# Loading the first attention head's rows in chunks 13 and 14 of the preparation, its values copied on chip

## What is computed

```python
xn = _layernorm(x)
# attention
q = _rope(split(xn @ Wq + bq)); k = _rope(split(xn @ Wk + bk)); v = split(xn @ Wv + bv)
scores = einsum('bhnd,bhmd->bhnm', q, k) / sqrt(d)
inter = einsum('bhnm,bhmd->bhnd', softmax(scores), v)
attn = inter.transpose(0, 2, 1, 3).reshape(b, n, d) @ Wo + bo
# feed-forward with weights of +1 and -1
h = s0 * (concat([xn, -xn]) @ pm(k0)); h = 2 * relu(h)
h = s1 * (h @ pm(k1)); h = 2 * relu(h)
ffn = s2 * (h @ pm(k2))
return x + attn + ffn
```

## Time and profile before

| | us |
|---|---|
| median of 3 runs | 2652.44 (2651.83 to 2652.5) |
| the profiled execution | 2653.31 |
| its span | 2651.5 |
| the preparation, to the first scores of attention | 0 to 235.6 |
| TensorE busy in the span | 2574.1 (97%) |
| ScalarE busy | 2099.2 (79%) |
| VectorE busy | 977.0 (37%) |
| GpSimd busy | 299.5 (11%) |
| DMA, first tenth of the span | 0.8 to 0.9 busy, 280 to 301 GB/s in the first three slices |
| DMA, later | 0.1 to 0.2 busy |

### The profile page before, as it was taken

How to read it: one execution, slowest core, us unless ns; L and a number is a source line. 1 busy time by engine, 2 the same in 40 slices (tenths; PEclk the granted TensorE clock), 3 DMA queues, 4 the chain that set the end, 5 groups by cost and what they waited for, 6 DMA issues and landing times.

```text
span 2651.5 us, 49117 instructions
## 1 busy us (share of the span) xinstructions
PE 2574.1 (97%) x20679; PEld 1337.6 (50%) x20679; DVE 977.0 (37%) x1669; ACT 2099.2 (79%) x2341; POOL 299.5 (11%) x268
## 2 busy tenths in 40 slices
PE   7887999999999999999999999999999999999997
PEld 5664454544445454545445454545445454545444
DVE  7774233243423332233423332233423332233422
ACT  6885888888888878787887878787887878787883
POOL 6774000000000000000000000000000000000000
PEclk9998999999999999999999999999999999999998
DMA  8995111121212122122212122122212112122203
GB/s 280 301 295 164 41 48 55 45 60 53 58 46 72 46 61 65 52 68 60 77 46 76 47 60 65 52 69 61 77 46 74 49 54 71 51 70 61 77 26 115
DMA packets 235414, 211.83 MB, mean 80 GB/s; under 512 B 146860, under 2 KB 191676, under 8 KB 228792
## 3 DMA queue, kind: packets, MB, share of 16 engines
q1 hardware_dynamic: 226744, 200.29, 25.5%
q10 hardware_dynamic: 8448, 8.39, 1.0%
HBM read 132.06 MB, written 76.55 MB: 79 GB/s over the span
## 4 chain that ended last, share of the span: by engine, by line
PE 89%; issue 1%; DMA 0%; DVE 0%; ACT 0%; SPq 0%; POOLq 0%; POOL 0%; PEldq 0%; ACTq 0%
PE ps_o L1012 36%; PE ps_f L1045 27%; PE ps_s L999 24%; PE ps_y L1058 2%; PE ps_f L1095 0%; DMA probs<-rest_sum_d 0%; PE ps_y L1095 0%; PE ps_o L1095 0%; ACT probs L979 0%; DVE sums L1133 0%; DMA heads_t<-heads 0%; DVE h_lo L1168 0%; POOLq L821 0%; DVE raw L1157 0%; ACT L979 0%
## 5 line engine op out<-in xcount | busy, mean ns | idle before, releaser
L979 ACT ACTIVATE probs<-ps_s 128x1024 f32<-128x1024 f32 x2048 | 1929.8, 1033 | 445.6 <-PE ps_s L999 443.5
L1012 PE MATMUL ps_o<-probs,v_ones 128*32 128x512 f32 x8192 | 1011.4, 600 | 0.0
L999 PE MATMUL ps_s<-q_rows,k_rows 50*128 50x512 f32 x4096 | 868.7, 439 | 6.7 <-SPq L948 5.4
L999 PEld LDWEIGHTS ps_s<-q_rows,k_rows 50*128 50x128 f32 x4096 | 365.9, 184 | 675.6 <-ACT probs L979 601.5
L1012 PEld LDWEIGHTS ps_o<-probs,v_ones 128*32 128x32 f32 x8192 | 201.2, 109 | 417.3 <-issue 294.7
L1045 PE MATMUL ps_f<-h_hi,ffn_w 64*128 64x512 f32 x2048 | 409.2, 393 | 0.0
L1045 PE MATMUL ps_f<-h_lo,ffn_w 64*128 64x512 f32 x2048 | 408.2, 391 | 0.0
L1157 DVE COPY raw<-ps_f 128x512 f32<-128x512 f32 x256 | 164.8, 686 | 560.6 <-PE ps_f L1045 560.6
L1112 POOL TENSOR_TENSOR heads<-heads,sums 128x512 f32<-128x512 f32 x64 | 82.2, 1284 | 2141.0 <-DVE sums L1133 2141.0
L1133 DVE RECIPROCAL sums<-sums 128x128 f32<-128x128 f32 x256 | 226.6, 923 | 1.7
L1045 PEld LDWEIGHTS ps_f<-h_lo,ffn_w 64*128 64x128 f32 x2048 | 198.0, 187 | 34.7
(11 more groups left out here) (105 smaller groups left out, 1376.2 us busy)
## 6 DMA issues: line engine op xcount, KB each, us to landing
k_rows<-k_parts SPq DMA_DIRECT2D x128, 256.0 KB
q_rows<-q_parts SPq DMA_DIRECT2D x384, 64.0 KB
q_parts<-parts SPq DMA_DIRECT2D x32, 512.0 KB, 8.5
k_parts<-parts SPq DMA_DIRECT2D x32, 512.0 KB, 8.5
k_rows<-k_parts SPq DMA_DIRECT2D x128, 128.0 KB
x_chunk<-in_x ACTq DMA_DIRECT2D x16, 512.0 KB, 9.5
xn_d<-xn_t SPq DMA_DIRECT2D x16, 512.0 KB, 9.1
v_heads<-v_sb SPq DMA_DIRECT2D x16, 512.0 KB, 8.1
```

The source lines that it names most:

```text
L979: nc.scalar.activation(probs[:, s % PBUF, half * 2 * C:(half + 1) * 2 * C], ps_s[:, half].rearrange("p c n -> p (c n)"), ACT.Exp, scale=SC ...
L999: last = nc.tensor.matmul(ps_s[:, half, w], k_rows[rows, u, t * P:(t + 1) * P], q_rows[rows, u, half], start=True, stop=True)
L1012: last = nc.tensor.matmul(ps_o[32 * c:32 * c + 2 * DH], v_ones[:, u, t], probs[:, s % PBUF, c * C:(c + 1) * C], start=(t == 0), stop=(t == ...
```

## The change

`FIRST_HEAD_AT` goes from 6 to 13. In chunk 13 SP issues the two zero rows and then all five loads of half 0; in chunk 14 the five loads of half 1 and the load of `xT_lo`. The biases are loaded in chunk 5. The four value loads are gone: at the end of chunks 1 to 4 VectorE copies head 0's values out of `v_sb` into `v_ones`, and ScalarE waits for that copy (`v_kept`) before it writes the `v_sb` buffer again. The memset of ones beside them moves on GpSimd from chunk 6 to chunk 4. The bound is written into another buffer, the second half of `q_rows`, and its four stores are counted on a semaphore of the whole program; the preparation no longer waits for them, attention's SP does, ahead of head 1's loads. ScalarE ends the preparation with an exponential of one column.

```diff
-FIRST_HEAD_AT = 6
+FIRST_HEAD_AT = 13
+        bound_fill = w["q_rows"][:, 1, 0, 0:FILL]
@@ prepare, SP
             def load_first(c):
                 if c == FIRST_HEAD_AT:
                     sp.wait_ge(k_rows_set, 1)
-                at = c - FIRST_HEAD_AT
-                if 0 <= at < LOADS - 2:
-                    load_rows(sp, scratch, 0, w["q_rows"][:, 0], w["k_rows"][:, 0], first_loaded, only=at)
-                if at == 1:
                     for w_half in range(2):
-                        row_of_bound(1, w_half, zero_row)
-                if at == 2:
-                    sp.wait_ge(ones_set, 1)
-                if at % 2 == 0 and 2 <= at < 2 + 2 * CB:
-                    r = at // 2 - 1
-                    v_src = scratch["v"].rearrange("c p (h t d) -> c p h t d", h=H, t=TT)
-                    sp.dma_start(w["v_ones"][:, 0, r * TT:(r + 1) * TT, 0:DH], v_src[r, :, 0]).then_inc(first_loaded, 16)
-                if at == 3:
+                        row_of_bound(1, fill[:], w_half, zero_row)
+                if FIRST_HEAD_AT <= c < FIRST_HEAD_AT + 2:
+                    load_rows(sp, scratch, 0, w["q_rows"][:, 0], w["k_rows"][:, 0], first_loaded, only=c - FIRST_HEAD_AT)
+                if c == FIRST_HEAD_AT + 1:
+                    sp.dma_start(w["xT_lo"][:].bitcast(F32).rearrange("p k n -> p (k n)"), scratch["xn"][0]).then_inc(first_x_loaded, 16)
+                if c == FFN_WEIGHTS_AT + 1:
                     sp.dma_start(bv[:], a["bv"].rearrange("(k p) -> p k", p=P), allow_slow_non_contiguous=True).then_inc(bias_loaded, 16)
                     sp.dma_start(bo[:], a["bo"].rearrange("(o n) -> o n", o=1).broadcast_to([P, D])).then_inc(bias_loaded, 16)
-                if at == 5:
-                    sp.dma_start(w["xT_lo"][:].bitcast(F32).rearrange("p k n -> p (k n)"), scratch["xn"][0]).then_inc(first_x_loaded, 16)
...
-                row_of_bound(0, w_half, bound_row)
-            store_shift(0)
-
-            sp.wait_ge(first_loaded, 16 * (LOADS - 2 + CB))
-            sp.wait_ge(fill_stored, 2 * FILLS)
+                row_of_bound(0, bound_fill, w_half, bound_row)
+            store_shift(0, bound_fill, bound_stored)
+
+            sp.wait_ge(first_loaded, 16 * (LOADS - 2))
+            sp.wait_ge(fill_stored, FILLS)
@@ prepare, ScalarE
                     act.wait_ge(v_stored[u], 16 * (c // 2))
+                    act.wait_ge(v_kept, min(c - 1, CB))
...
             nc.scalar.activation(bound[:], bound2[:], ACT.Sqrt).then_inc(bound_ready, 1)
+            nc.scalar.activation(std[:, 0, 0:1], eps[:], ACT.Exp)
@@ prepare, GpSimd
-                if n == 4 * FIRST_HEAD_AT:
+                if n == 4 * FFN_WEIGHTS_AT:
                     pool.wait_ge(d0_ready, 1)
-                    nc.gpsimd.memset(w["v_ones"][:, :, :, DH:2 * DH], 1.0).then_inc(ones_set, 1)
+                    nc.gpsimd.memset(w["v_ones"][:, :, :, DH:2 * DH], 1.0)
@@ prepare, VectorE
+                dve.wait_ge(v_done, 2 * NC)
-                nc.vector.tensor_scalar(fill[:], fill[:].bitcast(F32), bcol[:, 0:1], None, ALU.add).then_inc(fill_ready, 1)
+                nc.vector.tensor_scalar(bound_fill, fill[:].bitcast(F32), bcol[:, 0:1], None, ALU.add).then_inc(fill_ready, 1)
...
+                    dve.wait_ge(d0_ready, 1)
+                if 1 <= c <= CB:
+                    dve.wait_ge(v_ready, 2 * c)
+                    nc.vector.tensor_copy(w["v_ones"][:, 0, (c - 1) * TT:c * TT, 0:DH], v_sb[:, (c - 1) % 2, 0]).then_inc(v_kept, 1)
@@ attend, SP
             sp.sem_inc(v_loaded[0], 16 * CB)
+            sp.wait_ge(bound_stored, FILLS)
+            sp.sem_inc(turn_begun, 1)
             load_head(1, 1)
```

More of the change, by code:

```diff
@@ L133, in exists, with prepare @@
     return not last_batch or r + n < CB
-def prepare(nc, a, w, scratch):
+def prepare(nc, a, w, scratch, bound_stored):
     ctx = ExitStack()
@@ L246, in prepare @@
         k_rows_set = sem("k_rows_set")
-        ones_set = sem("ones_set")
+        v_kept = sem("v_kept")
         wo_loaded = sem("wo_loaded")
@@ L270, in _, with store_shift @@
         def _(sp):
-            def store_shift(a):
+            def store_shift(a, filled, landed):
                 to = scratch["shift"][a].rearrange("g (h w n) -> w (g h) n", h=P // G, n=FILL)
                 for n in range(G * N // (P * FILL)):
-                    sp.dma_start(to[n], fill[:].bitcast(F32)).then_inc(fill_stored, 16)
+                    sp.dma_start(to[n], filled.bitcast(F32)).then_inc(landed, 16)
             sp.dma_start(ident[:], a["ident"]).then_inc(ident_loaded, 16)
@@ L290, in _ @@
             sp.wait_ge(zero_ready, 1)
-            store_shift(1)
+            store_shift(1, fill[:], fill_stored)
             def store_x(c):
@@ L303, in store_parts, with row_of_bound @@
                 sp.dma_start(to, parts[:, u].bitcast(F32)).then_inc(parts_stored[u], 16)
-            def row_of_bound(n, w_half, landed):
+            def row_of_bound(n, filled, w_half, landed):
                 at = GROUP_ROWS * w_half + AUG + n
                 to = w["q_rows"][at:at + 1, 0].bitcast(F32).rearrange("p h (m n) -> p (h m) n", n=FILL)
-                row = fill[0:1].bitcast(F32).rearrange("p (o n) -> p o n", o=1)
+                row = filled[0:1].bitcast(F32).rearrange("p (o n) -> p o n", o=1)
                 sp.dma_start(to, row.broadcast_to([1, N // 2 // FILL, FILL])).then_inc(landed, 16)
@@ L705, in _, with maxima @@
             nc.vector.tensor_tensor(bo[:], bo[:], ps_p[:, 0, 0, 0:D], ALU.add)
-def maxima(nc, w, scratch):
+def maxima(nc, w, scratch, bound_stored):
     ctx = ExitStack()
@@ L802, in load_rows @@
         here = slice(w * N // 2, (w + 1) * N // 2)
-        if only in (None, 5 * w):
+        if only in (None, w):
             sp.dma_start(k_rows[at:at + 2 * DH, :].bitcast(F32), k_head[g]).then_inc(loaded, 16)
-        if only in (None, 5 * w + 1):
             sp.dma_start(k_rows[at + 2 * DH:at + AUG, :].bitcast(F32), k_head[g, 0:2]).then_inc(loaded, 16)
-        if only in (None, 5 * w + 2):
             sp.dma_start(q_flat[at:at + DH].bitcast(F32), q_head[g, 0:2, :, here]).then_inc(loaded, 16)
-        if only in (None, 5 * w + 3):
             sp.dma_start(q_flat[at + DH:at + 2 * DH].bitcast(F32), q_head[g, 0:2, :, here]).then_inc(loaded, 16)
-        if only in (None, 5 * w + 4):
             sp.dma_start(q_flat[at + 2 * DH:at + AUG].bitcast(F32), q_head[g, 2:4, :, here]).then_inc(loaded, 16)
@@ L814, in load_rows, with attend @@
             sp.dma_start(q_flat[at + AUG:at + ROWS].bitcast(F32), shift[g, w]).then_inc(loaded, 16)
-def attend(nc, a, w, scratch, out):
+def attend(nc, a, w, scratch, out, bound_stored):
     ctx = ExitStack()
@@ L1237, in layer @@
         }
-        prepare(nc, a, w, scratch)
-        maxima(nc, w, scratch)
-        attend(nc, a, w, scratch, out)
+        bound_stored = ctx.enter_context(nc.semaphore("bound_stored"))
+        prepare(nc, a, w, scratch, bound_stored)
+        maxima(nc, w, scratch, bound_stored)
+        attend(nc, a, w, scratch, out, bound_stored)
 def tables():
```

## The result

The changed kernel takes **2660.38 us**, median of eight executions (2659.22 to 2662.76), against 2652.41 for the kernel before (2651.55 to 2653.04) on the same chip. The ratio is 1.0032, 95% interval 1.0023 to 1.0041: slower by 8.0 us, past the 0.2% of the prediction's own bound. I had forecast 2655.2, no change; the time lies 5.2 us above that, within the stated range of 2644 to 2664. The profiled execution took 2661.25 us, its span 2659.5, against 2653.31 and 2651.5.

A forecast was written before the change was run, and what follows sets the result against it. DMA was taken to bound chunks 6 to 12, DMA and GpSimd together the last three. Terms -5.3 + 9.1 - 0.8 - 0.4 + 0.2 = +2.8 us gave 2655.2 us, range 2644 to 2664.

The forecast's parts named there:

- The row loads' price: Chunks 13 and 14: ten row loads moved there take 17.0 us on two DMA engines, 8.5 us per half head.
- the queue on two engines: All row loads use the same two DMA engines in order, 54 GB/s; wide transfers land only after their share there.
- relief: Chunks 13 to 15: engines move data faster while the others stand still, taking 4.4 us off the added cost.
- The single loads that they replace: Chunks 13 to 15: three 64 KB loads that stood there go, crediting 3.6 us.
- the tail: Chunks 13 to 15: added loads less idle DMA and faster engine pace, +9.1 us, bounds +3.3 and +13.5.
- Chunks 6 to 12: Middle of the preparation: 1.61 MB of loads removed at 302 GB/s gives -5.3 us, bounds -2.9 to -10.8.
- The end: End of the preparation: SP's wait for the shift stores goes, -0.8 us.
- the values: Four VectorE copies of 128x64 at 0.2 us each; only the one in chunk 1 costs, +0.2 us.
- the table: Start of attention: exponential table loaded earlier, in ScalarE's idle end, -0.4 us, between 0 and -0.6.
- The slower one: Rival, chance 0.33: two engines' queue without faster pace; chunks 13 to 15 cost +13.5, middle gives 2.9; +9.6 us, 2662.0.
- The bytes rival: Rival, chance 0.17: bytes are the limit, not two engines; last chunks +3.3, middle -10.8; total -8.5 us, 2643.9.
- The hidden burst: Rival, chance 0.08: loads not queued as read, or one burst hidden in chunks 13 to 15; 2648 to 2651 us.

## Why the prediction came out as it did

**The row loads' price: right.** The mechanism was that of the prediction, the queue on two engines. Of its signs, the waits of over 5 us for part stores came (7.40 and 8.75); the DMA share fell to 0.85, where I had said well under 0.9; the landings were 12.7 to 15.4 us, where I had said 15 and more. Of 17.0 us of engine time I let 1.6 go into idle DMA and 4.4 into relief, which leaves 11.0; the rows cost 10.7. The sum is confirmed, its two deductions are not: no run takes them apart. The Trainium skill's rule (DMA: Bandwidth & Descriptors, Why a DMA increments its semaphore by 16 and not by 1), that a DMA runs on the largest count up to 16 that divides the slowest dimension of both sides, agrees with what splitting into 8-row pieces gave back, 5 us at equal bytes.

**The single loads that they replace: mis-sized.** I credited the tail with 3.6 us for three 64 KB loads, their time on the two engines. They cost 1.4, and 0.1 counted from ready part to first bound row. With 10.7 for the rows, 1.2 for the x load and zero rows (40.22 - 39.00, where I had 1.7; one small value load is missing on that side) and -1.4, the tail is +10.5 instead of +9.1.

**Chunks 6 to 12: the step that failed.** "I take the bytes, which lie nearest to the saturated chunk." -5.3 was forecast; -1.5 came by the table's marks and -2.8 by those of ready parts, which are the forecast's own marks in the kernel before. So about a quarter to a half came, at best the smallest gain that I allowed, 2.9. I read DMA's 0.99 and ScalarE's waits for part stores as one limit and divided bytes by the rate. ScalarE's waits for part stores did fall by 7.9 us, but 4.4 of it came back as waits for GpSimd and 2.0 as a wait for VectorE, and I had priced neither. Removing 1.0 MB of single loads gave 1.1 us (2.3 by the other marks), adding 3.67 MB cost 5.0 by both. My sign "still at 90 us would prove that their bytes cost nothing" was badly chosen: first store to first store the stretch takes 91.30 us, and what fills it up is SP's hold of 3.7 us on a ready part, where I had expected the store 1.4 us late.

**The end, the values, the table.** -0.8 was -1.0 (and 0.8 alone, 6.80 against 7.61). The values' copy was mis-sized: the first takes 0.20 us, as taken, but the three others 0.90 to 0.92, VectorE's rows say. Chunk 6 starts 0.04 later, so they cost nothing that shows; over the kernels of this study that start varies by more than 1.5 us, and a term of 0.2 can't be found in it. The table's 0.4 is there at the first exponential and not found at the end.

**The rivals.** The slower one gave 2662.0, nearest by number. Half of its reason held: its middle, -2.9, is what came by ready parts, while its tail of 13.5 us was too dear (10.5 or 11.8), since by it the rows alone would have cost 17.0 less 1.6, 15.4, and they cost 10.7. That something takes those 4.7 us off is measured; that it is the faster pace of two engines while the others stand still fits in size (4.4) and wasn't tested. The time lies in the range because this rival set its upper end, not because my own sum held: so far it is luck. Its remark on TensorE's clock came true, with no price that shows. After the window in which TensorE worked 11.20 of 17.56 us, the granted clock is 0.50, the 1.2 GHz level, from 222.33 to 236.77; but GpSimd is 9.81 of 9.84 us busy in the first part of that, ScalarE waits 0.4 us for TensorE from 187 to 236 us, and the kernel before is at 0.50 too from 223.15 to 227.76. The bytes rival falls with splitting, with the kernel that has the bursts alone, and with the one that has none. The hidden burst falls with the bursts at chunk 6.

## What to carry to other kernels

A busy share of 0.99 isn't a bound: before dividing bytes by a rate, add up the waits for the resource on the engine that is next, since hardly more than these can come back, and price the waits between the other engines that then show: here 8.3 us of such waits gave 1.5 to 2.8. Compare a stretch by a mark that the change doesn't move, or by two marks. Narrow transfers are cheap one at a time and dear in a row: what counted here is the run of narrow work in front of a wide store whose buffer someone waits for, not the total. If they must come together, split them over more engines; here that gave back 5 of 8 us.

## What the runs showed of the hardware

- Wide transfers issued behind a run of narrow ones land late: 12.7 to 15.4 us for 512 KB behind five row loads, where the median before was 8.5. With the rows in ScalarE's queue the waits for SP's stores were still 13.1 us, against 9.9 without bursts.
- Behind a burst two engines are still at work when the others have nothing left: share 0.15 at 58 GB/s from 220.30 to 222.30 us, 17 us after the last row load was issued (202.65).
- The issue of one and the same store isn't of constant length: SP's issue of the x store took 3.75 us at 207.66, behind the second burst, and 0.47 in most chunks. With the bursts alone moved the same issue took 2.11, and in the kernel before it once took 2.37 with no burst, from SP's timeline, so the bursts are not shown to be the only cause:

```profile
180.52 2.37 SPq L296 DMA_DIRECT2D xn_d<-xn_t  x1
```

- The DMA busy share of a stretch was 1.00 at 296 GB/s and 1.01 at 319.
- The same VectorE copy of 128x64 took 0.20 us at 48.92 and 0.90 to 0.92 at 59.13, 70.56 and 85.62; why wasn't looked into.
